# Reordering the start-up of a fused attention and feed-forward kernel, one mask product a head, and transposed scores in 384 columns

## The reference, cut to what matters

```python
scores = einsum('bqhd,bkhd->bhqk', q, k) * scale
scores = where(pos[None, :] <= pos[:, None], scores + slopes * rel, -1e9)
attn = softmax(scores, axis=-1)
```

## Time and profile before

| | us |
|---|---|
| median of three runs | 1350.14 |
| the profiled execution | 1351.68 |
| its span | 1349.9 |
| TensorE busy | 1222.1 |
| VectorE busy | 777.9 |
| ScalarE busy | 520.9 |
| GpSimd busy | 353.7 |

### The profile page before, as it was taken

The page is one execution under the profiler, slowest core; times in us unless marked ns, Lnnn a source line. Parts: engine busy times, 40 slices in busy tenths (PEclk is TensorE's granted clock), DMA queues, the critical chain, the costliest instruction groups (busy, mean ns, idle before and its releaser), DMA issues.

```text
span 1349.9 us, 21318 instructions
## 1 busy us (share of the span) xinstructions
PE 1222.1 (91%) x7656; PEld 681.7 (50%) x7656; DVE 777.9 (58%) x1173; ACT 520.9 (39%) x698; POOL 353.7 (26%) x203
## 2 busy tenths in 40 slices
PE   2686679999999999999999999999999999999988
PEld 2353225655455545556355555556356555555436
DVE  5675553558644684457734684458725586356822
ACT  0332046323543255332643245332643236342562
POOL 3075293047000920038000830028000650000000
PEclk9889569999999999999999999999899999999999
DMA  6788723267043732267043642258042650348024
GB/s 252 227 289 330 179 72 75 61 165 219 18 110 131 175 120 58 56 172 230 23 110 122 161 142 48 66 162 241 22 110 96 139 191 15 97 148 231 18 110 172
DMA packets 81063, 180.99 MB, mean 134 GB/s; under 512 B 14468, under 2 KB 54356, under 8 KB 71284
## 3 DMA queue, kind: packets, MB, share of 16 engines
q1 hardware_dynamic: 76144, 166.81, 42.6%
q10 hardware_dynamic: 3552, 8.67, 1.7%
q0 software_dynamic: 1280, 4.20, 0.8%
HBM read 106.41 MB, written 21.14 MB: 94 GB/s over the span
## 4 chain that ended last, share of the span: by engine, by line
PE 71%; DVE 8%; SPq 7%; DMA 5%; issue 3%; ACT 3%; POOL 3%; DVEq 0%; ACTq 0%; POOLq 0%
PE psum L1151 9%; PE psum L1103 9%; PE psum L929 7%; PE psum L969 6%; SPq L413 5%; PE psum L970 4%; PE psum L971 4%; PE psum L958 4%; PE psum L1063 4%; PE psum L947 3%; PE psum L935 3%; DVE max L837 3%; PE psum L1138 3%; PE psum L1027 3%; PE psum L1043 2%
## 5 line engine op out<-in xcount | busy, mean ns | idle before, releaser
L837 DVE TENSOR_REDUCE max<-psum 128x1 f32<-128x512 f32 x512 | 327.7, 684 | 119.9 <-PE psum L1103 116.7
L675 ACT ACTIVATE probs<-psum 128x1024 f32<-128x1024 f32 x256 | 247.9, 1022 | 174.5 <-PE psum L1138 173.2
L1103 PE MATMUL psum<-k,q 52*128 52x512 f32 x512 | 187.1, 507 | 34.1 <-DMA k<-low 20.6
L546 POOL TENSOR_TENSOR h<-h_in,tap 128x1024 f32<-128x1024 f32 x7 | 13.3, 1897 | 606.4 <-DVE low L741 606.4
L1103 PEld LDWEIGHTS psum<-k,q 52*128 52x128 f32 x512 | 78.2, 194 | 167.9 <-DVE max L837 126.0
L1151 PE MATMUL psum<-probs,v 128*32 128x512 f32 x1024 | 140.3, 621 | 0.4 <-ACT probs L675 0.3
L1138 PE MATMUL psum<-q,k 54*128 54x512 f32 x512 | 114.1, 443 | 15.6 <-DMA q<-max_l 8.1
L556 POOL TENSOR_TENSOR h<-h,products 128x1024 f32<-128x1024 f32 x49 | 121.8, 2485 | 3.8
L969 PE MATMUL psum<-stack 128*128 128x512 f32 x256 | 113.7, 444 | 0.0
L739 DVE CAST high<-low 128x1024 fp32r<-128x1024 f32 x32 | 22.9, 716 | 143.5 <-ACT low L575 116.3
L929 PE MATMUL psum<-h,qkv_w 128*128 128x256 f32 x448 | 103.5, 384 | 0.0
(11 more groups left out here) (114 smaller groups left out, 1743.2 us busy)
## 6 DMA issues: line engine op xcount, KB each, us to landing
stack<-wd_sorted SPq DMA_DIRECT2D x64, 1024.0 KB, 6.6
stack<-high SPq DMA_DIRECT2D x128, 128.0 KB, 2.4
stack<-low SPq DMA_DIRECT2D x64, 128.0 KB, 2.4
q<-high SPq DMA_DIRECT2D x128, 64.0 KB, 4.2
k<-high SPq DMA_DIRECT2D x128, 64.0 KB, 2.5
h_in<-in_x_lanes SPq DMA_DIRECT2D x9, 512.0 KB, 3.9
x<-in_x_rows SPq DMA_DIRECT2D x8, 512.0 KB, 7.6
wd_sorted<-q SPq DMA_DIRECT2D x4, 1024.0 KB, 8.8
```

What stands on the lines that cost most here:

```text
L675: nc.scalar.activation(probs[:, u // 2 % 2, u % 2 * 2:u % 2 * 2 + 2, :], psum[:, 2 + u % 2 * 2:4 + u % 2 * 2, :], ACT.Exp)\
L837: nc.vector.reduce_max(max2[:, g, e, i, t:t + 1], psum[:, SCORE_BANKS[s], :], AX_X).then_inc(S["s2_max"], 1)
L1103: nc.tensor.matmul(psum[:, SCORE_BANKS[s], :], r(q2[rows, g, i, t * P:(t + 1) * P]), r(k2[rows, g, i, :]), start=True, stop=True).then_inc ...
```

## The change

1. **First loads.** ScalarE's first loads wait until x, the taps and the convolution's bias have landed; SyncE's loads from the segment masks on wait for the last piece of query and key weights. Chunk 0 of the gate and up tables waits for the natural stores, as chunk 1 did.
2. **Sorting.** There are eight buffers, four of them in the tiles of the first attention's stacks. Pieces 4 to 7 are gathered after the last transposed score, copied by ScalarE behind the query evacuation, subtracted by VectorE after the key split, and stored by SyncE between stack groups 1 and 2. The stacks of batch 0 wait only for pieces 0 to 3; the fixed rows of the next item wait for pieces 4 to 7. Chunk loads 3 to 7 move to ScalarE's queue. The maxima rows of group 0 go ahead of stack group 3 in batch 0.
3. **Batch 0.** The first 28 window scores use four PSUM banks in turn.
4. **Masks.** One product of 256 columns a head in either kind of score. In the first scores it writes blocks 0 and 3 of the bank's four; block 1 is not read by the maximum.
5. **Transposed scores.** The second product's moving operand starts 128 columns later, so its first 128 columns are the queries wanted and the other 128 are of the next head and are not used. The exponential reads and writes 384 columns a head in place of 512.
6. **Tail.** moments(2) goes ahead of gate_up(1), and ScalarE loads the silu table before the first z copies.

```diff
-SORT = 4
+SORT = NT
+EARLY = 4
+FIRST_BANKS = [(0, 1, 3, 4)[s % 4] if s < WINDOW_SCORES - 4 else SCORE_BANKS[s] for s in range(NS)]
...
+        stacked = stack1[:].rearrange("p s a g n -> p (s a g n)")
...
-                      .rearrange("p (a g n) -> p a g n", a=2, g=2) for t in (q2, k2) for i in range(2)]
+                      .rearrange("p (a g n) -> p a g n", a=2, g=2) for t in (q2, k2) for i in range(2)] \
+            + [stack1[:, i] for i in range(NT - EARLY)]
...
             def load_chunk(c):
                 u, q = c // 4, c % 4
-                if c == 0:
-                    sp.wait_ge(second_out, NQ)
-                elif c == 1:
+                if c < 2:
                     sp.wait_ge(natural_stored, 16 * NQ)
...
+            sp.wait_ge(qk_loaded[CT - 1], 16)
             for i in range(2):
                 sp.dma_start(seg_words[i].bitcast(I32), seg_mask[:, i * 1024:(i + 1) * 1024]).then_inc(seg_loaded, 16)
...
-            for n in range(SORT):
-                store_sorted(n)
-            for c in range(3, 5):
-                load_chunk(c)
-            for n in range(SORT, NT):
+            for n in range(EARLY):
                 store_sorted(n)
...
                     stacks2(g)
-                    if first and g < 3:
-                        load_chunk(5 + g)
+                    if first and g == 1:
+                        for n in range(EARLY, NT):
+                            store_sorted(n)
+                    if first and g == 2:
+                        max_rows(b, 0)
...
-                max_rows(b, 0)
                 if first:
                     sp.wait_ge(gate_up_step, 3 * N_GEN)
                     sp.dma_start(zt[:], z_table).then_inc(zt_loaded, 16)
+                    for k in range(EARLY, NT):
+                        sp.wait_ge(sorted_stored[k], 16)
                 else:
+                    max_rows(b, 0)
...
             for c in range(3):
                 gate_up_chunk(c)
-            for n in range(SORT, NT):
+            pool.wait_ge(S["t1_ready"], H1 // 2)
+            for n in range(EARLY, NT):
                 gather(n)
...
         @block.scalar
         def _(act):
+            act.wait_ge(S["x_loaded"], 16)
+            act.wait_ge(conv_loaded, 32)
...
-                    nc.scalar.activation(probs[:, g % 2, p % 2 * 2:p % 2 * 2 + 2, :],
-                                         psum[:, 2 + p % 2 * 2:4 + p % 2 * 2, :], ACT.Exp).then_inc(S["p1_out"], 1)
+                    nc.scalar.activation(probs[:, g % 2, p % 2 * 2:p % 2 * 2 + 2, 0:L + P],
+                                         psum[:, 2 + p % 2 * 2:4 + p % 2 * 2, 0:L + P], ACT.Exp)\
+                        .then_inc(S["p1_out"], 1)
                 if first:
-                    for n in range(SORT, NT):
-                        sort_high(n)
+                    for c in range(3, 5):
+                        load_chunk(c)
...
                 if first:
+                    for n in range(EARLY, NT):
+                        sort_high(n)
                     act.wait_ge(ones_made, 2)
...
-                if not first:
+                if first:
+                    for c in range(5, N_GEN):
+                        load_chunk(c)
+                else:
                     feed(b)
...
             batch(B - 1, last=True)
+            nc.scalar.activation(warm[:], ones[:, 0:1], ACT.Silu)
             moments_out(B)
...
                 for t in range(LT):
-                    for n in range(SORT + 2 * t, SORT + 2 * t + 2) if first else ():
-                        sort(n)
                     wait("proj_ready", t + 1)
...
                 split(b, 1, "high2", "low2")
+                for n in range(EARLY, NT if first else EARLY):
+                    sort(n)
...
-                    nc.tensor.matmul(bank[:, 0:L], ident_b[:], mask_q[:], start=False, stop=False,
-                                     skip_group_check=True)
-                    last = nc.tensor.matmul(bank[:, L + P:2 * L], ident_b[:], mask_q[:, 0:P], start=False, stop=True,
+                    last = nc.tensor.matmul(bank.rearrange("p (t n) -> p t n", n=P)[:, 0:4:3, :], ident_b[:],
+                                            mask_q[:, None, :].broadcast_to([P, LT, P]), start=False, stop=True,
                                             skip_group_check=True)
...
                             nc.tensor.matmul(bank[:, t * L:(t + 1) * L], r(k1[0:END1, i, t * P:(t + 1) * P]),
-                                             r(q1[0:END1, i, :]), start=t == 0, stop=False, skip_group_check=True)
-                        nc.tensor.matmul(bank[:, 0:P], ident_b[:], mask_k[:, P:2 * P], start=False, stop=False,
-                                         skip_group_check=True)
-                        last = nc.tensor.matmul(bank[:, L:2 * L], ident_b[:], mask_k[:], start=False, stop=True,
+                                             r(stacked[0:END1, i * L + t * P:(i + 1) * L + t * P]),
+                                             start=t == 0, stop=False, skip_group_check=True)
+                        last = nc.tensor.matmul(bank.rearrange("p (t n) -> p t n", t=LT)[:, :, 0:P], ident_b[:],
+                                                mask_k[:, None, :].broadcast_to([P, LT, P]), start=False, stop=True,
                                                 skip_group_check=True)
...
-                        if not first:
+                        if first:
+                            wait("s2_max", WINDOW_SCORES - 4)
+                        else:
                             pe.wait_ge(S["inter_out"], fed(b, "inter_out", NT))
...
             gate_up(B, 0)
+            moments(B, AHEAD)
             for n in range(NT):
                 if n + 1 < NT:
                     gate_up(B, n + 1)
-                for m in range(AHEAD if n == 0 else n + AHEAD + 1, min(n + AHEAD + 2, NT)):
-                    moments(B, m)
+                if n + AHEAD + 1 < NT:
+                    moments(B, n + AHEAD + 1)
```

More of the change, by code:

```diff
@@ L800, in sort @@
                                             sort_slots[n % SORT][:, 0], ALU.subtract).then_inc(down_low, 1)
-                for n in range(SORT if first else 0):
+                for n in range(EARLY if first else 0):
                     sort(n)
@@ L1087, in scores @@
                 def scores(s):
+                    banks = FIRST_BANKS if first else SCORE_BANKS
+                    last_in_bank = (FIRST_LAST_IN_BANK if first else LAST_IN_BANK)[s]
                     g, n = s // GS, s % GS
```

51 lines of the change are left out of this document (28 added, 23 removed).

## The result

The changed kernel took 1322.72 us in the median of four runs (1319.5 to 1324.0), the kernel before beside it 1350.58. The ratio is 0.9766, interval 0.9734 to 0.9798. The change makes the kernel 28 us faster. I had forecast 1287 in a range of 1274 to 1310, so the sign is right and the size less than half: 64 us were forecast. The profiled execution took 1323.93 us around a span of 1322.0, 27.9 less than before.

What follows compares the result with a forecast made beforehand. TensorE was taken to bound the steady batches, with a relay of waits in the start-up and batch 0. Start-up and batch 0 -46.4, masks -15 and tail -3 sum to -64.4 from 1351.7: 1287, range 1274 to 1310.

Steps and rivals of the forecast that it cites:

- Natural stores at 54.7: Start-up: first products 17.8 us earlier and chunk 0 waiting (-1.7) bring gathers, before at 74.2, forward by 19.5 us.
- waits only for the projection: Batch 0: with late sorting moved away, the residual add gains 7.7 us and ends at 92.1 instead of 120.0.
- Without the wait for the stores the stacks start as in a steady batch: Batch 0, SyncE's queue: first score 17.2 us after the add instead of 24.8, -7.6, so at 109.2.
- Window 22.4: Batch 0's second-attention scores: four banks give pairs of 1.40 us, 32 scores in 22.4 us, ending at 131.6.
- rival A: Store burst in SyncE's queue delays stack group 2 and maxima rows, which land near 140: +8, 1295; chance 0.14.
- GpSimd has chunk 7 at about 119: Batch 0: at 4.3 to 5.7 us a chunk, the next convolution ends at 154, before TensorE wants it at 162.
- rival E: Batch 0: chunk 7 after 130, or half clock through the rounds: +10, 1297; chance 0.09.
- Masks and exponentials, -2.1 a batch: First attention: mask products save 1.0 us in first scores and 0.6 in transposed ones, shorter exponentials 0.5.
- The steady part's sum, -15 for seven batches: Seven steady batches each gain 2.1 us from masks and exponentials; bounds 0 and -3 a batch.
- Tail -3: End of kernel: Silu table load under the last outputs, moments(2) into a wait; -3 us, bounds -1.3 and -4.
- Rival B: Steady part covered by VectorE's maxima and value products, so nothing of the 15 us comes: 1302; chance 0.12.
- Rivals C and D: C: slow small loads, convolution at 14, +8, 1295, chance 0.08. D: mask products 0.35 us dearer, 1364, chance 0.02.

Runs made afterwards that it cites:

- e3: Changed kernel with GpSimd's residual and mask rows held until the natural copies are made; 1320.72 us.
- e15: e8 plus six unread products a batch; gathers 4 to 7, chunk loads 5 and 6 held until stack group 0 landed; sorting copies and subtractions later; 1312.57 us.
- e6: Changed kernel with item 0's window taken back from four score banks to two; 1322.79 us.
- e8: Changed kernel with GpSimd's residual and mask rows held, sorted stores 4 to 7 behind stack group 3, group 1's maxima rows before chunk 7's wait; 1313.67 us.
- e11: Kernel before with the new order of the first loads alone; 1343.45 us.

## Why the prediction was wrong, step by step

**First loads: right.** Forecast: convolution from 6.3, first products done at 27.0, copies from 29.7. Measured 5.5, 28.2, 30.9. Taking four microseconds for conv_bias was near (3.1).

**Natural stores at 54.7: missed by 8.3.** "GpSimd's products end just in time" looked at who waits for GpSimd and not at whom GpSimd slows. The rows were at hand: the convolution's first 8 instructions took 7.7 us beside GpSimd and the last 8 took 4.0. I credited that difference as a gain and didn't ask what the moved work would lie beside next. It lay beside the split, 7.8 us instead of 3.8, and TensorE, idle meanwhile, fell to half clock for the loop (4.7 us a piece instead of 3.8). The Trainium skill (GPSIMD Engine Reference, Specifications) has the rule: GpSimd and VectorE contend at their memory interface in certain forms of instruction; the cast's 2.38 against 0.69 us agrees. And "chunk 0 waits: -2.7": the last store took 10.3 us against 11.0 before, and 13 in e3. So keeping chunk 0 away bought 0.7 us and not 2.7.

**Residual add "waits only for the projection": right**, 21.3 us earlier against 27.9 forecast, the 6.6 short being the step above. (The recorded 92.1 is also 0.5 off its own parts: 19.5, 1.2 and 7.7 taken from 120.0 leave 91.6.)

**"Without the wait for the stores the stacks start as in a steady batch", -7.6: missed whole.** They do start then, but 24.4 us passed as before. The wait for the stores had kept the DMA engines free for the stacks (busy 0.38 of the time from 130 to 142 in the kernel before); without it the stacks share them with 2 MB of gathers and the loads of chunks 4 and 5 (busy 1.06 from 98 to 110). e15 shows large transfers as the cause. I had the late gathers as covered because nobody waits for them, and counted only issue time for chunk loads on another queue. The Trainium skill (DMA: Bandwidth & Descriptors, Issuing engines are not separate DMA queues) says that all issuers' transfers run on the same 16 engines and interleave. e15 agrees with 5.6 us; I had cited a neighbouring rule of that page and not this one.

**Window 22.4: right in size (21.0) by luck.** The first shifted score stands ahead of the last pair, so 30 scores count and not 32. They took 17.8 us, pairs of 1.22 and not 1.4, and 3.2 us of waiting for the maxima rows, rival A's sign, filled the rest. Of the 9.3 us that I gave to the banks, 2.0 are theirs; the rest belongs to the rows' place in the queue, as e6 shows.

**"GpSimd has chunk 7 at about 119", before TensorE wants it: wrong by 32 us**, and with it batch 0's end. I added GpSimd's own 4.3 to 5.7 us a chunk and took the loads as hidden. Those of chunks 4 to 6 took 20 to 24 us for a megabyte, beside gathers, stacks and stores. This was rival E's first half and rival A's transfer, together, and with the steps above larger than either price (10 and 8): 25.5 of the 46.4 us didn't come. A had the right traffic and looked at the wrong follower: the maxima rows landed at 141 to 144, but the chunks behind the stores set the end. With the chain relieved (e8), item 1 starts 11.5 us earlier.

**Masks and exponentials, -2.1 a batch: right**, -12.5 us in two stages over six batches, 2.1 each. Exponentials of 0.81 us, as taken. (The 12.6 us named as a sign for the transposed stage doesn't follow from the working, which takes 1.1 from 14.7; it measured 13.5.) **The steady part's sum, -15 for seven batches: wrong**, since 10 of those 12.5 us came back as half clock. I had looked at the clock for batch 0 alone and never priced it where it stood at full. That the place is a weak one was to be read in the kernel before: two of its batches lost the clock there, with the same waits. The Trainium skill (TensorE: Matmul & The Clock Gate, A second HAM failure mode: psum-queue depth-cycling) tells of a kernel whose frequent short idle times between groups of products make the clock swing. The rows agree: no single wait here was over 1.2 us. The rule that I cited in the prediction spoke only of the way back to full.

**Tail -3: right within its bounds.** From the tail's first moments to the end it was 48.1 us and is 44.2, so 3.9, part of it 3 us of half clock that the kernel before had at 1309. Batch 7 itself gave 0.4 of its 2.1. The table load now lies at the end of batch 7:

```profile
1276.28 1.28 ACT L728 ACT_TABLE_LOAD   x1
...
1280.88 0.60 ACT L604 ACTIVATE probs<-psum 128x512 f32<-128x512 f32 x1 [0.72 <-PE psum L984]
```

Rival B (nothing of the steady part, 1302) came nearest in effect, but not in mechanism: the two stages did get shorter. Rivals C and D are out: the convolution started at 5.5, and the new mask products take 0.28 us like the old ones of 256 columns. The range failed because its high end joined B with one late transfer, and what happened was most of B's price, two late transfers that followed each other, and the slower split.

**Open.** Why, among batches with the same waits, one keeps its clock and the next loses it, and why the mask edit, which takes nothing from the rounds, makes the fall at their start more frequent. e11 suggests that it changes with the start of the batches, and no run here separates that further.

## What to carry to other kernels

Where a wait is removed, ask what it kept off the DMA engines: here it had kept them free for the very transfers it seemed to delay, and 1 MB loads that nobody waited for became the chain. A price for removed TensorE work holds only if its clock holds: read the granted clock at every place where TensorE already waits, and where it falls in any batch, try products, useful or not, in the wait. And when work moves, look up what it slowed where it was, and find the same kind of neighbour where it goes.

## What the runs showed of the hardware

Six products of 128x512 a batch whose result nobody reads made the changed kernel 12 us faster and the kernel before 5. In the changed kernel the fall to 1.2 GHz lasted 3 or 7 us at the rounds' start and cost 1.3 to 2.6 us; at the turn it lasted 3 us and cost about 1, with another 0.3 in the stage behind. A kernel whose batches merely began 14 us earlier had it in five batches instead of two, in one profiled execution of each (e11). A VectorE cast of 128x1024 took 0.69 us alone and 2.38 beside a GpSimd sum of the same shape (e3 and the changed kernel). From 110 to 120 us in the changed kernel the DMA engines were busy 0.94 of the time and moved 206 GB/s:

```profile
110.00:120.00 10.00, 0.00 (x0) 0.00 (x0) 4.24 (x4) 2.15 (x5) 3.11 (x2) 0.63 0.94 206
```

In the same ten microseconds of the kernel before, with other traffic, they moved 408 GB/s at a share of 1.06:

```profile
110.00:120.00 10.00, 5.34 (x9) 1.75 (x7) 6.74 (x6) 4.23 (x4) 5.43 (x4) 0.83 1.06 408
```

So a busy share near one doesn't say how much gets through.
